# A Mamba, attention and expert block: the delta bias as a row of the product, and the second pair's taps behind the first pair's halves

## The reference

```python
xh, z = jnp.split(xz, 2, axis=-1)                      # 192 channels each
xc = conv_general_dilated(xc, conv_w, ..., feature_group_count=DI)   # 3 x 3 per channel
xc = jax.nn.silu(xc + conv_b[None, :, None, None])
x_dbl = jnp.einsum('bkdl,kcd->bkcl', xs, x_proj_w)     # four directions k
dts, Bs, Cs = jnp.split(x_dbl, [R, R + N], axis=2)     # R = 24, N = 16
dts = jnp.einsum('bkrl,kdr->bkdl', dts, dt_projs_w)
dts = jax.nn.softplus(dts + dt_projs_b[None, :, :, None])
out_y = selective_scan(xs, dts, As, Bs, Cs, Ds)        # h = h * exp(d*A) + d*u*B
```

## Time and profile before

| what | us |
|---|---|
| median of 3 runs | 2245.13 |
| lowest and highest | 2244.14, 2249.29 |
| span of the profiled execution | 2244.7 |
| delta stage, first L1621 to first L1688 | 103.99 to 253.46 |
| VectorE and ScalarE busy in 104 to 253.5 | 127.70 and 125.96 |
| span of the profiled execution less the median | -0.4 |

### The profile page before, as it was taken

One profiled execution on the slowest core, in us unless ns is written; L12 is line 12 of the kernel. 1 busy time (PEld: TensorE's weight loads), 2 busy tenths in 40 slices (PEclk: granted clock), 3 DMA queues, 4 the chain that ended last, 5 costly groups with the idle time before them and its releaser, 6 DMA issues.

```text
span 2244.7 us, 20167 instructions
## 1 busy us (share of the span) xinstructions
PE 1984.1 (88%) x5826; PEld 919.6 (41%) x5830; DVE 1575.2 (70%) x1505; ACT 1144.9 (51%) x1258; POOL 1297.0 (58%) x464
## 2 busy tenths in 40 slices
PE   7988588888888888888888888989995999999997
PEld 3332133333333333333333333456653555555554
DVE  6978999999999999999999999774553000000000
ACT  4788666666776676776767666211213112122111
POOL 0110499999999999999999999401233011111110
PEclk9987599999999999999999999999997999999999
DMA  6448622233222233222232220611226233333300
GB/s 193 151 175 280 212 75 75 70 98 79 84 66 65 75 100 91 65 75 75 61 105 67 77 73 19 229 42 57 85 85 223 85 119 124 123 119 126 126 24 7
DMA packets 82402, 229.13 MB, mean 102 GB/s; under 512 B 14031, under 2 KB 40257, under 8 KB 80816
## 3 DMA queue, kind: packets, MB, share of 16 engines
q1 hardware_dynamic: 76208, 211.54, 29.6%
q0 software_dynamic: 6144, 16.98, 2.1%
HBM read 166.39 MB, written 64.03 MB: 103 GB/s over the span
## 4 chain that ended last, share of the span: by engine, by line
PE 46%; DVE 23%; issue 17%; POOL 8%; ACT 3%; DMA 1%; DVEq 0%; SPq 0%; ACTq 0%; POOLq 0%
DVE arena L1705 15%; PE ps L1489 11%; PE ps L1502 11%; PE ps L1229 6%; POOL arena L604 4%; POOL arena L587 4%; PE ps L1439 3%; PE ps L1213 2%; PE ps L1110 2%; DVE ps L1688 1%; PE ps L1226 1%; PE ps L1139 1%; PE ps L1390 1%; PE ps L1428 1%; DVE arena L1572 1%
## 5 line engine op out<-in xcount | busy, mean ns | idle before, releaser
L604 POOL TENSOR_TENSOR arena<-arena 128x2048 f32<-128x2048 f32 x192 | 868.3, 4533 | 16.6 <-DVE arena L1705 15.7
L1229 PE MATMUL ps<-arena 128*128 128x512 f32 x1536 | 727.7, 596 | 27.7 <-POOL arena L604 27.6
L1705 DVE TENSOR_TENSOR_SCAN arena<-arena,ps 128x1024 f32<-128x1024 f32 x264 | 587.5, 2266 | 0.0
L880 ACT ACTIVATE arena<-ps 128x1024 f32<-128x1024 f32 x384 | 390.7, 1017 | 248.0 <-PE ps L1213 246.1
L1213 PE MATMUL ps<-arena 96*128 (+1 forms) x1296 | 366.7, 384 | 129.3 <-DVE arena L1705 112.7
L1229 PEld LDWEIGHTS ps<-arena 128*128 128x128 f32 x1536 | 288.4, 190 | 287.7 <-issue 194.0
L587 POOL TENSOR_TENSOR arena<-arena 128x1024 f32<-128x1024 f32 x120 | 283.1, 2359 | 103.5 <-DMA arena<-b_rows 103.5
L2066 DVE TENSOR_TENSOR arena<-ps,arena 128x384 f32<-128x384 f32 x32 | 17.8, 557 | 450.4 <-PE ps L1502 450.4
L1688 DVE TENSOR_TENSOR ps<-ps,arena 128x1024 f32<-128x1024 f32 x264 | 309.1, 1216 | 12.6 <-PE ps L1213 12.6
L873 ACT ACTIVATE arena<-arena 128x1024 f32<-128x1024 f32 x264 | 300.8, 1139 | 8.9 <-DVE arena L1705 8.3
L1213 PEld LDWEIGHTS ps<-arena 96*128 96x128 bf16 x1296 | 112.9, 98 | 461.3 <-DVE arena L1705 215.7
(11 more groups left out here) (225 smaller groups left out, 1611.9 us busy)
## 6 DMA issues: line engine op xcount, KB each, us to landing
arena<-b_rows SPq DMA_DIRECT2D x240, 256.0 KB, 4.2
arena<-in_w SPq DMA_DIRECT2D x16, 2304.0 KB, 13.3
delta<-arena SPq DMA_DIRECT2D x24, 512.0 KB, 2.9
delta_x<-arena SPq DMA_DIRECT2D x24, 512.0 KB, 3.1
arena<-delta SPq DMA_DIRECT2D x24, 512.0 KB, 3.6
arena<-delta_x SPq DMA_DIRECT2D x24, 512.0 KB, 4.6
slot_in<-arena SPq DMA_DIRECT2D x8, 772.0 KB, 8.1
arena<-slot_in SPq DMA_DIRECT2D x8, 772.0 KB, 18.0
```

The costliest lines, as they stand in the source:

```text
L604: nc.gpsimd.tensor_tensor(hst[:, h:h + 2], hst[:, h:h + 2], c_sb[:, c:c + 2], ALU.mult).then_inc(p2_ok, 2)
L880: nc.scalar.activation(c_sb[:, u % RING], C_PS, ACT.Copy).then_inc(c_free, 1)
L1229: mm = pe.matmul(Y_PS[:, h * 512:(h + 1) * 512], ident, hst[:, u % HRING, h * 512:(h + 1) * 512], start=False, stop=(u == UN - 1))
L1705: nc.vector.tensor_tensor_scan(h, f, x, 0.0, ALU.mult, ALU.add).then_inc(sc_ok, 1)
```

## The change

The bias of delta becomes a 49th row of the weights `dt_w`, brought by two DMAs of single elements (the array holds it across partitions), and `rows` gets a 49th row of ones: the copy out of PSUM (L737) takes one more partition, and a bias of one on the row that is zero. `dt_bias` is no longer loaded as a column. With the bias in the product, ScalarE takes the absolute value without one, the biased copy L768 goes, and the new `whole_delta` on VectorE reads the product itself from PSUM. So a product now waits for `pd_ok` (whole_delta of two halves before) in place of `dtev_ok`. ScalarE adds the one for every half, and takes the logarithm of half s - 1 ahead of the exponential of half s. On VectorE whole_delta of half s - 1 stands ahead of the lost part of half s. Of the second pair's 20 taps on VectorE six stand ahead of the first half and two behind each of the first seven steps. The SiLU goes from step 6 to step 8, and two x_proj one step later.

Core of the diff:

```diff
-SILU_AT = 6
-DT_ROWS_AT = {(0, 2): (0, 1), (0, 8): (1, 0), (1, 1): (1, 1)}
-BC_ROWS_AT = {(0, 0): (0, 0), (0, 5): (0, 1), (0, 10): (1, 0), (1, 3): (1, 1)}
+SILU_AT = 8
+TAPS_FIRST, TAPS_A_STEP = 6, 2
+DT_ROWS_AT = {(0, 2): (0, 1), (0, 9): (1, 0), (1, 1): (1, 1)}
+BC_ROWS_AT = {(0, 0): (0, 0), (0, 5): (0, 1), (0, 11): (1, 0), (1, 3): (1, 1)}
...
             sp.dma_start(dt_w[H2:H2 + DR], a["dt_w"]).then_inc(ld_c, 16)
+            for lo in (DR, H2 + DR):
+                sp.dma_start(dt_w[lo:lo + 1], a["dt_bias"].rearrange("p q r one -> one q r p"),
+                             allow_slow_non_contiguous=True).then_inc(lb_ok, 16)
...
-                nc.scalar.activation(rows[0:H2 + DR, o], fill_slot("xd", p, o)[0:H2 + DR], ACT.Copy).then_inc(rows_ok, 1)
+                nc.scalar.activation(rows[0:H2 + DRB, o], fill_slot("xd", p, o)[0:H2 + DRB], ACT.Identity,
+                                     bias=one_row[0:H2 + DRB]).then_inc(rows_ok, 1)
...
-            def dt_out(p, i):
-                k, j, q, dr = half_of(p, i)
+            def absolute(p, i):
                 m = p * HALVES + i
-                bias = dt_bias[:, q % OJ, dr, :]
                 act.wait_ge(dt_ok, m + 1)
                 if m >= MADE:
                     act.wait_ge(dm_st[m % MADE], m // MADE * 32)
+                elif m == 0:
+                    act.wait_ge(xc_ok, J)
                 elif m == BLANK_FROM:
                     act.wait_ge(zero_st, 16 * E)
-                nc.scalar.activation(u_mk[:, m % MADE], DT_PS[m % 2], ACT.Abs, bias=bias).then_inc(ab_ok, 1)
-                nc.scalar.activation(d_mk[:, m % MADE], DT_PS[m % 2], ACT.Identity, bias=bias).then_inc(dtev_ok, 1)
+                nc.scalar.activation(u_mk[:, m % MADE], DT_PS[m % 2], ACT.Abs).then_inc(ab_ok, 1)
...
                     if s < HALVES:
-                        dt_out(p, s)
-                        exp_abs(p, s)
-                        if s % J == 0:
-                            one_more(p, s)
+                        absolute(p, s)
                     if s >= 1:
                         log_w(p, s - 1)
+                    if s < HALVES:
+                        exp_abs(p, s)
+                        one_more(p, s)
...
                 if m >= 2:
-                    pe.wait_ge(dtev_ok, m - 1)
+                    pe.wait_ge(pd_ok, m - 1)
+                elif m == 0:
+                    pe.wait_ge(lb_ok, 32)
                 for h in range(2):
-                    mm = pe.matmul(DT_PS[m % 2][:, h * 512:(h + 1) * 512], dt_w[lo:lo + DR, q % OJ, dr],
-                                   rows[lo:lo + DR, k % 2, h * 512:(h + 1) * 512], start=True, stop=True)
+                    mm = pe.matmul(DT_PS[m % 2][:, h * 512:(h + 1) * 512], dt_w[lo:lo + DRB, q % OJ, dr],
+                                   rows[lo:lo + DRB, k % 2, h * 512:(h + 1) * 512], start=True, stop=True)
...
             def lost_part(p, i):
 
                 m = p * HALVES + i
                 u, w = u_mk[:, m % MADE], w_mk[:, m % 2]
-                if i % J:
...
-                    chain.link(nc.vector.tensor_scalar(w, u, 1.0, None, ALU.add))
-                else:
-                    dve.wait_ge(w_ok, m // J + 1)
+                dve.wait_ge(w_ok, m + 1)
                 nc.vector.scalar_tensor_tensor(out=u, in0=w, scalar=-1.0, in1=u, op0=ALU.add, op1=ALU.subtract).then_inc(lost_ok, 1)
 
+            def whole_delta(p, i):
+
+                m = p * HALVES + i
+                dve.wait_ge(ln_ok, m + 1)
+                nc.vector.scalar_tensor_tensor(out=d_mk[:, m % MADE], in0=DT_PS[m % 2], scalar=0.0, in1=w_mk[:, m % 2],
+                                               op0=ALU.max, op1=ALU.add).then_inc(pd_ok, 1)
+
...
                 for s in range(HALVES + 1):
+                    if s >= 1:
+                        whole_delta(p, s - 1)
+                    if p == 0 and s == 0:
+                        for n in range(TAPS_FIRST):
+                            second_pair_tap(n)
+                        done = TAPS_FIRST
                     if s < HALVES:
                         lost_part(p, s)
                     if s >= 1:
                         finish(p, s - 1)
...
+                    if p == 0:
+                        upto = min(done + TAPS_A_STEP, taps_of_pair)
+                        for n in range(done, upto):
+                            second_pair_tap(n)
+                        done = upto
```

More of the change, by code:

```diff
@@ L25 @@
 DR = 2 * R
+DRB = DR + 1
 SR = 2 * N
@@ L182, in hybrid_block_kernel @@
         a_neg = always.take(OJ, 2, N)
-        dt_bias = always.take(OJ, 2, 1)
+        one_row = always.take(1)
         d_sum = always.take(OJ, 1)
@@ L363, in hybrid_block_kernel @@
         CONSTS = [
-            (ident, "ident"), (ones, "ones"), (a_neg, "a_logs"), (dt_bias, "dt_bias"), (d_two, "ds"),
+            (ident, "ident"), (ones, "ones"), (a_neg, "a_logs"), (d_two, "ds"),
             (conv_b, "conv_b"), (norm_g, "norm_g"), (norm_b, "norm_b"),
@@ L1262, in _ @@
             pe.wait_ge(rows_ok, 2 * NP)
-            pe.wait_ge(dtev_ok, NP * HALVES)
+            pe.wait_ge(pd_ok, NP * HALVES)
             tile_steps(0, True, False)
@@ L1577, in taps, with whole_tap @@
                         chain.link(ins)
[L1579 removed]
+            def whole_tap(j, tap):
                 acc = xy[:, OJ + j, :].rearrange("p (h w) -> p h w", w=HW)
[L1582 to L1591 removed]
@@ L1593, in last_taps @@
-            def last_taps(j):
-                slot = fill_slot("conv", 1, j).rearrange("p (h w) -> p h w", w=HW)
-                dve.wait_ge(cpe_ok, 1)
-                for tap in range(PE_TAPS, TAPS):
-                    dy, dx = divmod(tap, 3)
-                    last = tap == TAPS - 1
-                    acc = xy[:, OJ + j, :].rearrange("p (h w) -> p h w", w=HW) if last else slot
-                    ins = nc.vector.scalar_tensor_tensor(out=acc, in0=xpad[:, j, dy:dy + HW, dx:dx + HW], scalar=conv_w[:, j, tap:tap + 1],
-                                                         in1=slot, op0=ALU.mult, op1=ALU.add)
-                    if last:
-                        ins.then_inc(conv_ok, 1)
-                    else:
-                        chain.link(ins)
+                dy, dx = divmod(tap, 3)
@@ new lines, in whole_tap @@
+                if tap == 0:
+                    dve.wait_ge(xh_ok, IN_ORDER.index((3, j)) + 1)
+                    chain.link(nc.vector.tensor_scalar(acc, xpad[:, j, 0:HW, 0:HW], conv_w[:, j, 0:1], None, ALU.mult))
+                    return
+                ins = nc.vector.scalar_tensor_tensor(out=acc, in0=xpad[:, j, dy:dy + HW, dx:dx + HW], scalar=conv_w[:, j, tap:tap + 1],
+                                                     in1=acc, op0=ALU.mult, op1=ALU.add)
+                if tap == TAPS - 1:
+                    ins.then_inc(conv_ok, 1)
+                else:
+                    chain.link(ins)
@@ new lines, in last_tap @@
+            def last_tap(j, tap):
+                slot = fill_slot("conv", 1, j).rearrange("p (h w) -> p h w", w=HW)
+                if tap == PE_TAPS:
+                    dve.wait_ge(cpe_ok, 1)
+                dy, dx = divmod(tap, 3)
+                last = tap == TAPS - 1
+                acc = xy[:, OJ + j, :].rearrange("p (h w) -> p h w", w=HW) if last else slot
+                ins = nc.vector.scalar_tensor_tensor(out=acc, in0=xpad[:, j, dy:dy + HW, dx:dx + HW], scalar=conv_w[:, j, tap:tap + 1],
+                                                     in1=slot, op0=ALU.mult, op1=ALU.add)
+                if last:
+                    ins.then_inc(conv_ok, 1)
+                else:
+                    chain.link(ins)
@@ L1608, in lost_part, with second_pair_tap @@
+            def second_pair_tap(n):
+                j, tap = divmod(n, TAPS)
+                if j < J - 1:
+                    whole_tap(j, tap)
+                else:
+                    last_tap(j, PE_TAPS + tap)
             def lost_part(p, i):
```

32 lines of the change are left out of this document (4 added, 28 removed).

## The result

The kernel after takes 2294.42 us (median of 4 runs, 2293.65 to 2295.6), the kernel before 2245.08 beside it: ratio 1.0217, 95% interval 1.0203 to 1.0232. It is 49 us slower, and 2296 was predicted.

What follows compares the result with a forecast made beforehand. Before, VectorE and ScalarE were nearly full; after, a closed loop of waits through TensorE, ScalarE and VectorE binds the delta stage. 107.7 + 194.6 + 2.5 = 304.8, 51.3 us later; 2244.7 + 51.3 = 2296, range 2262 to 2317.

Steps and rivals of the forecast that it cites:

- half 0 through: Delta stage, VectorE's whole_delta of the first half ends at 107.7 us, against 110.5 before.
- 7 plain turns: Delta-stage steps with nothing else standing in the queues: 7.3 us each, 51.1 in all.
- 6 with a split: Delta-stage steps with a split of B and C, its take and copy standing ahead of the absolute value: 9.4 us each.
- 4 with two taps: Steps of halves 2 to 5, at full clock and set by VectorE: 8.2 us each, 32.8 in all.
- 3 with x_proj: Steps where an x_proj stands between two products on TensorE: 9.3 us each, 27.9 in all.
- SiLU: One delta-stage step with the SiLU block: 9.4 us, two table loads and three activations, 15.2 us.
- 2 at a pair's end: Steps where no absolute value stands ahead of the logarithm on ScalarE: 5.6 us each, 11.2 in all.
- 23 steps: All delta-stage steps after half 0: 194.6 us, 8.5 a step against 6.1 before.
- first scan input: End of the delta stage: 304.8 us against 253.46 before, 51.3 us later.
- The ring: Delta stage: whole_delta, next product, absolute value, logarithm, whole_delta wait in turn; 7.3 us a turn at the low clock.
- The VectorE-bound rival: Delta stage held by VectorE's work, not by queue waits: stage ends at 234, 19 us earlier, 2225; chance 0.06.
- the rival priced: TensorE's clock stays at 1.00 in the delta stage: turns of 5.7 us, 18 us later instead of 51, 2263; chance 0.11.

Runs made afterwards that it cites:

- the last run above: Kernel before with additions of one shared out to ScalarE and taps and SiLU one half sooner, without the bias row: 2241.83 us, ratio 0.9987.
- two others: Kernel after with useless 128-row matmuls behind late products, 2291.09 us; kernel after with the logarithm behind the addition of one, 2325.91 us.

## Why the prediction was right

| its step | predicted | measured |
|---|---|---|
| half 0 through | 107.7 | 106.56 |
| 7 plain turns | 7.3 each | 7.16 |
| 6 with a split | 9.4 | 9.03 to 9.12 |
| 4 with two taps | 8.2 | 7.99 to 8.21, mean 8.1 |
| 3 with x_proj | 27.9 in all | 28.7 |
| SiLU | 15.2 | 15.0 |
| 2 at a pair's end | 5.6 | 5.66 |
| 23 steps | 194.6 | 191.8 |
| first scan input | 304.8 | 300.77 |

The ring is shown from both sides: cutting it by the copy gives 44 us back, closing it in the kernel before by a wait alone costs 97, and moving the logarithm changes the time with no instruction more or less, by 14 us down and 31 up. The VectorE-bound rival fell with its order of queues: VectorE is busy for 57 of the last 91 us. The clock was 1.00 from 130 to 155 us, beside taps and x_proj, and again beside each later x_proj (192 to 202 and 220 to 225 us, for example), so its mean from 160 us on is 0.60 and not the 0.50 that the prediction named. In all seven plain turns the product took 3.75 us, as forecast; where the upper level was forced, it gave the turn that the rival priced.

The time came nearer than the stage did, and that is luck. Of the stage 51.3 us more were forecast, and the profiles show 47.3: half 0 is through 1.1 us sooner than forecast, and the 23 steps are 2.8 us shorter. Between the medians it is 49.3, because the profiled executions aren't the medians: that of after took 2293.65 us, and that of before was late by half 0 already (whole_delta at 109.32; at 108.03 in the last run above, which has the same instructions up to there).

Two sizes were off. Whole_delta takes 1.22 us and not 1.28, and the absolute value without a bias 0.92 to the next start and not 1.0, which makes 7.16 of 7.3 in each turn. And the bias loads, costed at 0 behind a slack of 6.7 us, were not hidden: the text named a VectorE that waits at 37 us for constants as a sign against it, and VectorE does wait, 2.15 us. That sign was set too wide, since the wait hardly reached the stage here, but the price was wrong: the constants came at about 40 and not at 30.8, 9 us later where I had taken 3.6. The row price left out the queue: SP issues the first x_proj load only at 27.91 (before: 21.55). Not all of the 6.99 us ahead of it belongs to the single elements; in before SP stands in its last x_proj load until 28.01 too, but has issued the other three by then. In after all four come behind that, and their issuing takes 9.00 us (before: 6.46), to 36.91. From 28 to 32 us the DMA engines move almost nothing. SP's queue after, and three windows:

```profile
20.87 6.99 SPq L394 DMA_DIRECT2D arena<-in_dt_bias  x2
27.91 9.00 SPq L398 DMA_DIRECT2D arena<-in_xproj_w  x4
```

```profile
28.00:30.00 2.00, 2.00 (x6) 0.76 (x4) 1.86 (x4) 0.26 (x1) 0.00 (x0) 1.00 0.81 2
30.00:32.00 2.00, 2.00 (x10) 1.26 (x10) 1.70 (x8) 1.62 (x2) 0.00 (x0) 1.00 0.42 6
32.00:34.00 2.00, 2.00 (x6) 0.92 (x5) 2.00 (x4) 0.42 (x1) 0.00 (x0) 1.00 1.22 46
```

At 28 to 30 us the DMA engines are busy for 0.81 of the time at 2 GB/s. The estimate of 4.8 us that the prediction worked out from the Trainium skill ("DMA: Bandwidth & Descriptors", sections "Rules for kernel authors" and "Why a DMA increments its semaphore by 16 and not by 1") was also too low; the measurement decides. One descriptor per element fits the trace: after has 16983 packets under 512 bytes and before 14031, 2952 more. In this profile the wait hardly reached the end, since the first half waits for other work until 95 us; in two others the stage starts 5 us later, as shown above.

The placing got no price of its own in the prediction: the 14 taps stand inside the four tap steps. Alone it costs 6 us in the kernel before, and the copy put back leaves 5. How much of the 49 us it is inside the ring, no run tells apart.

## What to carry to other kernels

A buffer's release decides more than its fill: before a copy out of PSUM is dropped, follow the release from the last reader back through each in-order queue. If that path comes back to the same buffers and nothing in it can run ahead, add it up, with everything that stands in a queue ahead of a link: here that sum was the step time, whatever the busy shares said. The two rings that were added up wrongly, of the wait alone and of the logarithm first, had left out such instructions. The place of one instruction in one queue was worth 46 us (2280 to 2326) with the work unchanged. A copy that looks like waste may be what lets the producer run ahead.
